# One attention block's root refinement moves from GpSimd to VectorE, and the last group's transposes join those of the group before

## The reference

```python
q, k, v = split_heads(x @ Wq), split_heads(x @ Wk), split_heads(x @ Wv)   # 16 heads of 64
q, k = apply_rope(q), apply_rope(k)
sim = where(causal, einsum('bid,bjd->bij', q, k) * scale, -inf)
out = einsum('bij,bjd->bid', softmax(sim), v)
x = layernorm(x + out @ Wo + bo)
x = layernorm(x + moe(x))      # 8 experts, the top 2 of each token, GELU, then a layer norm inside
```

## Time and profile before

| | us |
|---|---|
| median of 3 runs | 816.63 (815.87 to 818.19) |
| the profiled execution, its device time | 816.16 |
| its span, first to last instruction | 814.4 |
| PE busy | 766.8 (94%) |
| DVE busy | 602.2 (74%) |
| ACT busy | 563.7 (69%) |
| POOL busy | 573.0 (70%) |

### The profile page before, as it was taken

The page is one execution under the profiler, slowest core; times in us unless marked ns, Lnnn a source line. Parts: engine busy times, 40 slices in busy tenths (PEclk is TensorE's granted clock), DMA queues, the critical chain, the costliest instruction groups (busy, mean ns, idle before and its releaser), DMA issues.

```text
span 814.4 us, 19400 instructions
## 1 busy us (share of the span) xinstructions
PE 766.8 (94%) x5259; PEld 548.5 (67%) x5259; DVE 602.2 (74%) x2144; ACT 563.7 (69%) x1616; POOL 573.0 (70%) x701
## 2 busy tenths in 40 slices
PE   8999999999999999999999999979998899999995
PEld 4555566666766566666666666656665579999995
DVE  6667677888798768978896688668876855225996
ACT  4577777777778767877677667756776656555676
POOL 4576767558776867696669776946686356999993
PEclk9899999999999999999999999999999999999998
DMA  4677778666866676767675756555568767434525
GB/s 145 192 238 222 220 230 246 212 214 207 249 194 222 194 207 198 221 213 219 205 224 177 221 171 217 185 181 190 193 195 235 234 195 204 118 85 126 161 86 159
DMA packets 146793, 158.85 MB, mean 195 GB/s; under 512 B 23616, under 2 KB 122432, under 8 KB 146688
## 3 DMA queue, kind: packets, MB, share of 16 engines
q1 hardware_dynamic: 133248, 147.73, 59.0%
q0 software_dynamic: 4224, 8.72, 3.3%
q10 hardware_dynamic: 9216, 1.17, 1.0%
HBM read 74.66 MB, written 46.20 MB: 148 GB/s over the span
## 4 chain that ended last, share of the span: by engine, by line
PE 65%; issue 8%; DVE 7%; DMA 7%; POOL 7%; SPq 4%; ACT 1%; DVEq 0%; ACTq 0%; POOLq 0%
PE AO L1158 12%; PE S_all L1119 9%; PE S_all L1327 7%; PE S_all L1138 6%; PE AO L1177 5%; PE AO L1340 3%; PE TB L1340 3%; DMA hT<-norms 3%; PE TB L1138 2%; DMA turns<-turned_pr 2%; PE TB L1119 2%; SPq L469 1%; PE AO L1054 1%; PE AO L1056 1%; SPq L621 1%
## 5 line engine op out<-in xcount | busy, mean ns | idle before, releaser
L1446 ACT ACTIVATE Pr_all<-Sm,nmax 128x512 f32<-128x512 f32 (+3 forms) x512 | 280.6, 554 | 89.0 <-DVE nmax L1684 88.5
L773 POOL TENSOR_TENSOR qk<-shared,qk 128x512 f32<-128x512 f32 x64 | 82.0, 1281 | 144.9 <-DMA qk<-shared 135.4
L1684 DVE CUSTOM_DVE_ANT_0 Sm<-S_all,causal 128x512 f32<-128x512 f32 (+2 forms) x384 | 170.8, 507 | 2.5 <-PE S_all L1119 2.3
L1158 PE MATMUL AO<-PT,shared 128*64 128x128 f32 x1008 | 153.9, 448 | 12.1 <-issue 10.1
L1119 PEld LDWEIGHTS S_all<-qk 64*128 64x128 f32 x768 | 69.8, 188 | 102.8 <-issue 86.6
L1119 PE MATMUL S_all<-qk 64*128 64x512 f32 (+2 forms) x768 | 129.5, 469 | 1.1 <-issue 1.0
L1158 PEld LDWEIGHTS AO<-PT,shared 128*64 128x64 f32 x1008 | 66.4, 139 | 62.2 <-issue 46.6
L1456 ACT ACTIVATE PT<-S_all 128x768 f32<-128x768 f32 (+1 forms) x129 | 70.1, 596 | 41.1 <-PE S_all L1138 41.1
L1446 ACT ACTIVATION_READ_ACCUMULATOR Pr_all<-Sm,nmax 128x1 f32 x512 | 98.3, 192 | 0.0
L847 POOL DMA_INDIRECT xrows<-pay,slot x64 | 65.6, 1025 | 33.7 <-issue 17.2
L1645 DVE TENSOR_TENSOR shared<-TB,cos_t 128x512 f32<-128x512 f32 x62 | 42.9, 691 | 61.8 <-PE TB L1056 31.0
(11 more groups left out here) (342 smaller groups left out, 1708.1 us busy)
## 6 DMA issues: line engine op xcount, KB each, us to landing
turns<-turned_pr SPq DMA_DIRECT2D x63, 512.0 KB
PT<-turns SPq DMA_DIRECT2D x252, 128.0 KB, 3.0
qk<-shared SPq DMA_DIRECT2D x124, 256.0 KB
hT<-norms SPq DMA_DIRECT2D x110, 128.0 KB
PT<-yrows SPq DMA_DIRECT2D x7, 512.0 KB, 4.2
w_tile<-in_wup SPq DMA_DIRECT2D x10, 256.0 KB, 3.3
xt<-xrows SPq DMA_DIRECT2D x32, 65.0 KB, 3.2
x_acc<-in_x SPq DMA_DIRECT2D x8, 256.0 KB, 3.9
```

What stands on the lines that cost most here:

```text
L773: nc.gpsimd.tensor_tensor(qT[p][:, :], q_cos, qT[p][:, :], ALU.add).then_inc(q_ready, 1)
L1158: last = nc.tensor.matmul(to, V[u // VS % 2][:, kb, u % VS * P + D * h:u % VS * P + D * h + D], pt_rows(p, h, kb), start=(kb == QB - 1), s ...
L1446: nc.scalar.activation(Pr[j][:, 0:n], Sm[j], ACT.Exp, bias=nmax[:, j:j + 1], scale=-1.0, accum_out=rsum[p][:, h * QB + qb:h * QB + qb + 1] ...
L1684: nc.vector.tensor_tensor_reduce(out=Sm[j], in0=score_bank(group, h)[:, at:at + n], in1=causal[:, T - n:T], scale=-0.125, scalar=HUGE, op0 ...
```

## The change

Two things are done.

**The root.** `refine_x1` goes. For every batch DVE refines the root, in n = 2, behind its two turns and ahead of `rope_q`: nine instructions (three steps of three) where POOL had twelve. POOL's `norm_half` waits for the last of them.

**The transposes.** T2 moves on PE from behind the projections of keys and values to right behind T1, and its copy on ACT from behind `keep_k` to ahead of it. T2 no longer goes to `TB` but to bank 3 of `S_all`. So it waits for six masks of the unit (which have read that bank) where it waited for all eight, and the users of bank 3 in n = 3, 4 and 7 wait for the copies too.

```diff
-NEWTON, STEPS = 3, 4
+NEWTON, STEPS = 3, 3
...
-            two = S_all[:, 0:2, :] if group == 1 else S_all[:, 2:4, :] if group == 2 and u == UNITS - 1 else TB
+            two = S_all[:, 0:2, :] if group == 1 else S_all[:, 3:4, :] if group == 2 else TB
...
-                if batch > 0 and n == NORM_AT:
-                    refine_x1(batch - 1)
...
-                    pe.wait_ge(maxed, BLK * (u + 2))
+                    pe.wait_ge(maxed, BLK * (u + 1) + DONE_BY[1])
...
                     pe.wait_ge(maxed, BLK * u + DONE_BY[1])
+                    pe.wait_ge(pt_ready, 2 * u)
...
                     transpose(u - 1, 1 - p, 1)
+                    transpose(u - 1, 1 - p, 2)
                 if 0 < u and u + 2 < UNITS:
                     project_k(u + 2, *second)
                 if 1 <= u <= VBLOCKS - QB:
                     project_v(QB + u - 1)
-                if not first:
-                    transpose(u - 1, 1 - p, 2)
...
                     copy_pt(u - 1, 1 - p, 1)
+                    copy_pt(u - 1, 1 - p, 2)
                 if u + 2 < UNITS:
                     keep_k(u + 2)
-                if not first:
-                    copy_pt(u - 1, 1 - p, 2)
...
-                done = NEWTON * STEPS * b + 3 * i
+                done = STEPS * (NEWTON * b + i)
...
+                if batch > 0 and n == NORM_AT:
+                    for i in range(NEWTON):
+                        refine_root(batch - 1, i)
```

More of the change, by code:

```diff
@@ L825, in add_bias @@
                 nc.gpsimd.tensor_tensor(part, part, bo_t[:, :].unsqueeze(1).to_broadcast([P, QB, C]), ALU.add).then_inc(x_set, 1)
[L827 to L839, removed]
             def rows_ready(b):
@@ L2019, in norm_rows @@
             def norm_rows(b):
-                dve.wait_ge(refined, NEWTON * (STEPS * b + 3))
+                dve.wait_ge(refined, NEWTON * STEPS * (b + 1))
                 dve.wait_ge(rows_sent[b % 2], 16 * QB * K * (b // 2))
```

## The result

| | before | after |
|---|---|---|
| median of 4 runs | 816.44 us | 827.26 us (825.69 to 828.76) |
| ratio after to before | | 1.0103, 95% interval 1.0059 to 1.0146 |
| span of the profiled execution | 814.4 | 823.9 |
| DVE busy | 602.2 | 628.3 |
| POOL busy | 573.0 | 557.7 |

The change costs 1.0%. The forecast was 826.0, the range 815 to 835. (The kernel before was run once more beside the change, so its median is 816.44 here, 0.19 less than above.)

The account below looks back on a forecast made before the run. The prediction took PE, with 65% of the chain of waits, to bound the kernel. Root 0, T2's wait 8 and key copy 1.3 made 9.3 on 816.16: 825.5, median 826 us, range 815 to 835.

Parts of the forecast that it names:

- The root, removed: POOL's twelve root instructions in n = 2 go; worth about 13 us if POOL alone caused the other lateness.
- The root, added: DVE's nine instructions in n = 2 are held by POOL's; pairs n = 3 and 4 total 153.2 against 154.41.
- The held instructions: Sign in n = 2: two to four of DVE's nine take up to 1.25 us, ending with POOL's.
- the units of n = 3 at about 11.4: Sign: first scores of n = 3 to the next unit's come about 11.4 us apart.
- the even pairs: Sign: pairs of n = 3 and 4 all last near 21.4 us rather than 19.5 to 24.2.
- The net of 0: Root as a whole, removed from POOL and added to DVE: 0 us, from -13 to +12.
- The faster rival: POOL decides, DVE's nine root instructions fall into POOL's holes: -3.2 us, 813.4; chance 0.14.
- T2's wait: T2 right behind T1 waits up to 0.50 us for mask 6; 18.4 us in all, 8 taken (2 to 18).
- the waits swallow each other: Rival: T2's wait falls where PE would wait anyway, 2 us; median 818.6, no change; chance 0.14.
- The key copy: ACT's key copy comes later, so POOL's `k_read` comes 0.6 us later: costs 1.3 us (0 to 4).
- four units that lose 0.3: Key copy: of 16 POOL waits, four units lose 0.3 us on average, the rest having spare at the load: 1.3.
- The worst rival: Everything late adds up: T2 14, PE's clock falling in n = 3 +6, key 2; 838.6 us; chance 0.14.

Follow-up runs that it names:

- `one_input`: Kernel before, with nine one-SBUF-input DVE instructions in place of the root (refinement left out in seven of eight batches): ratio 1.0026.
- `t2_after_k`: Kernel before, with T2 moved on PE between keys and values, into bank 3 of `S_all`; ACT's order unchanged: ratio 1.0005.
- `k_copy_first`: Kernel before, with T2 in bank 3 right behind T1 on PE, but the key copy still ahead of T2's copy on ACT: ratio 1.0039.
- `k_copy_last`: Kernel before, with T2 in bank 3 between keys and values on PE, and the key copy behind both transpose copies on ACT: ratio 1.0102.
- `turns_alone`: Kernel before, with only the transposes' part of the change (T2, its bank and its copy moved); POOL refines the root: ratio 1.0100.
- `root_psum`: Kernel before, with DVE refining the root in twelve instructions, one operand each in PSUM; transposes as before: ratio 0.9896.
- `root_alone`: Kernel before, with only the root's part of the change (nine instructions on DVE); transposes as before: ratio 1.0031.

## Why the prediction was right, and where its terms were not

**The time** (826.0 against 827.26) and the sign came out. The forecast had 0 for the root and 8 + 1.3 = 9.3 for the transposes; the parts alone measured 2.5 and 8.2. The second came out in total, with its two terms far off.

**The root, removed.** "If POOL alone were the cause of the rest, taking the root away would be worth about 13": the pairs gave 12.4, of which 4.4 was clock, and all runs together 8.3 (5.1 to 11.7). The cause is shown; the price was put too high.

**The root, added.** The held instructions, 3.7 to 4.5 us for the nine where the working had 4.0, the swap at about 11.9 (measured 11.57 in unit 18), the units of n = 3 at about 11.4 (median 11.39) and the even pairs came as forecast. The nine were through at 204.09, 200.2 in before's clock, where I had 200.4. `norm_o` came 1.9 later rather than 2.4 and T1 1.3 rather than 1.8. The net of 0 was 2.5 by itself (0.2 to 4.9). The faster rival ("the holding doesn't bind") falls. My reason for the hold was too narrow: it isn't two SBUF inputs, and `one_input` shows it. For this change that made no difference, since all nine have two.

**T2's wait.** The raw wait was forecast at 18.4 and measured 19.3, with 28 full units for 23. The step that failed is what stays of it: I took 8. Between `t2_after_k` and `k_copy_first` lie 2.8 us, by their intervals at most about 6, and those hold a key copy 0.3 later as well. So 8 was too much. The table of places suggests where it went: `attend` waited 12 us less, for a load that it would have awaited anyway. That is the rival "the waits swallow each other", right for this term and wrong for the whole.

**The key copy.** I put 1.3, at most 4. It measured 8.3 by itself (`k_copy_last`) and 5.0 on top of T2's wait (`turns_alone` against `k_copy_first`). Two steps failed. "POOL waited for it 16 times" takes one of the two rows of that wait, and only the units in which POOL stood waiting already. By the start of L778 against the end of the key copy, POOL took the key within 0.12 of its end in 25 of 59 units before, and within 0.72 in six more: 31 units, the number of waits of `k_copy_last`. And "four units that lose 0.3": 8.3 over 31 would be 0.27 in each of them, so it was the number of units that was mis-sized. I had looked for the loss at the load and found spare there. The traces agree that little is lost at the load, 0.5 of 7.5 us; the loss stands ahead of T1 and at the scores, which I hadn't priced. That the two terms' errors (5 too much and 4 to 7 too little) cancel is luck, and the forecast's total owes as much to it as to the reading.

**The worst rival** ("the clock falls in n = 3"): the clock in the seven pairs was 1.00 after, 0.93 in three of them before. It went the other way.

**Open:** how T2's wait and the late key share the loss when both are there. The intervals of `k_copy_first` and `turns_alone` overlap by a little (1.0064 to 1.0069), and no run had T2's wait with the key copy fully on time, since T2's matmuls stand ahead of the keys.

## What to carry to other kernels

When work moves from one engine to another, ask what the instruction's data share with the engine it now runs beside: nine small instructions in each of seven batches cost 12 us more beside a busy GpSimd with their data in SBUF than with them in PSUM, and in `root_psum` one operand in PSUM was enough. And when a step is made later, count the units in which its user comes at once or shortly after, not only the waits that the trace shows, and don't take the slack of one unit for the slack of a chain of units.

## What the runs showed of the hardware that was not expected

- A DVE instruction on four columns takes 0.16 us and, when it is held for one POOL instruction of 1.28, up to 1.27. Two in `root_alone` were passed over: one started at 438.90 while L784 ran and ended at 441.81, after L784, L778 and L779 had all ended (2.91 us), the other took 2.41. In the changed kernel one on 32 columns (L1797) took 3.62 beside three of POOL's. So POOL's next can come first.
- What was held: `tensor_tensor`, `scalar_tensor_tensor`, `tensor_scalar` and copies with all data in SBUF. What never was, in the changed kernel: anything with a PSUM operand (seven of the eight L1762 ran beside a POOL instruction, and all 61 readings of the query bank with a POOL instruction beside them took 0.69). Nor were the reductions to 4 columns, of which twelve of sixteen L1768 ran beside POOL; one other reduction (L1843) took 0.50 for 0.22 beside L996, and what held it stays open. The rows are the copy of 8 columns, the reduction to 4, and a `tensor_tensor` with `S_all`:

```profile
L1833 DVE COPY before_n<-before_n x8: 171/959/986, 183.4 to 690.7; 128x8 f32<-128x8 f32 x8
```

```profile
L1768 DVE TENSOR_REDUCE best<-placed x16: 186/186/186, 155.2 to 688.7; 128x4 f32<-128x32 f32 x16
```

```profile
L1762 DVE TENSOR_TENSOR lg<-S_all,ebias_t x8: 181/181/192, 143.7 to 684.1; 128x32 f32<-128x32 f32 x8
```
